# Gated attention stage: scores and gate as one product of 334 columns, key bias added on VectorE, mixing in two groups

## What is computed

```python
def _L1_xattn_ref(q, k, v, mask, Wq, bq, Wk, bk, Wv, bv, Wg, bg):
    q0 = q
    qp = q @ Wq + bq
    kp = k @ Wk + bk
    vp = v @ Wv + bv
    scale = 1.0 / jnp.sqrt(jnp.asarray(qp.shape[-1], qp.dtype))
    w = jnp.einsum('bqd,bkd->bqk', qp, kp) * scale
    w = jax.nn.softmax(w, axis=-1)
    x = jnp.einsum('bqk,bkd->bqd', w, vp)
    gate = jnp.concatenate((qp, x), axis=-1) @ Wg + bg
    x = x * mask[..., None]
    x = x * jax.nn.sigmoid(gate)
    return x + q0
```

## Time and profile before

| | us |
|---|---|
| median of the runs | 993.87 |
| span of the profiled execution | 989.4 |
| start of the last stage's first loads | 867.25 |
| the last stage, loads to end | 122 |
| TensorE, share of the span busy | 84% |
| VectorE / ScalarE / GpSimd | 68% / 43% / 47% |
| TensorE's mean granted clock | 0.909 |

### The profile page before, as it was taken

One profiled execution on the slowest core, in us unless ns is written; L12 is line 12 of the kernel. 1 busy time (PEld: TensorE's weight loads), 2 busy tenths in 40 slices (PEclk: granted clock), 3 DMA queues, 4 the chain that ended last, 5 costly groups with the idle time before them and its releaser, 6 DMA issues. The chain is left out here.

```text
span 989.4 us, 19663 instructions
## 1 busy us (share of the span) xinstructions
PE 831.0 (84%) x7264; PEld 678.2 (69%) x7264; DVE 677.2 (68%) x1459; ACT 430.4 (43%) x887; POOL 466.1 (47%) x584
## 2 busy tenths in 40 slices
PE   5974589998899988745778999989998989859997
PEld 4654467776677766434445888878877878859996
DVE  2633366766777776545689899999888887515664
ACT  3421135555555544422455555545443443234542
POOL 2003337766666764621234665655544556444440
PEclk9997799999999998856578999999999999958989
DMA  7293988796787771036435233323330000033333
GB/s 238 117 360 95 184 180 173 169 186 143 163 160 148 156 151 19 2 72 166 121 79 116 67 66 65 70 66 70 82 81 12 2 1 1 2 87 99 109 107 103
DMA packets 71102, 105.99 MB, mean 107 GB/s; under 512 B 21656, under 2 KB 60698, under 8 KB 66142
## 3 DMA queue, kind: packets, MB, share of 16 engines
q1 hardware_dynamic: 67092, 97.91, 42.4%
q10 hardware_dynamic: 3916, 6.83, 1.9%
HBM read 68.57 MB, written 35.62 MB: 105 GB/s over the span
## 5 line engine op out<-in xcount | busy, mean ns | idle before, releaser
L1329 DVE TENSOR_REDUCE a_nm<-a_s 128x2 f32<-128x512 f32 (+1 forms) x192 | 129.4, 681 | 86.2 <-PE a_s L1145 84.3
L1287 ACT ACTIVATE a_pT<-a_st 128x512 f32<-128x512 f32 x192 | 111.7, 594 | 111.1 <-PE a_st L1168 109.9
L975 POOL TENSOR_TENSOR c_hl<-c_hid,c_hh 128x256 fp32r<-128x256 f32 x128 | 95.0, 742 | 134.7 <-DVE c_hid L857 133.8
L686 ACT ACTIVATE c_pT<-c_st 77x512 f32<-77x512 f32 x128 | 76.0, 594 | 167.4 <-PE c_st L556 151.3
L606 PE MATMUL c_down<-c_w,c_hh 128*128 128x256 f32 x512 | 116.2, 295 | 2.9 <-DVE res L865 2.9
L1449 POOL TENSOR_SCALAR_AFFINE_SELECT a_pT<-a_pT 128x256 f32<-128x256 f32 (+1 forms) x192 | 89.7, 484 | 30.0 <-ACT a_pT L1287 29.7
L78 PE MATMUL c_up<-c_fxh,c_w 128*128 128x256 f32 x512 | 100.7, 289 | 0.7 <-DVE c_hid L857 0.6
L606 PEld LDWEIGHTS c_down<-c_w,c_hh 128*128 128x128 f32 x512 | 87.3, 191 | 18.0 <-issue 18.0
L1168 PE MATMUL a_st<-a_sq,a_sk 98*128 98x256 bf16 (+1 forms) x512 | 76.2, 253 | 16.0 <-DMA a_sq<-a_mT 11.6
L78 PEld LDWEIGHTS c_up<-c_fxh,c_w 128*128 128x128 f32 x512 | 79.9, 192 | 1.9 <-DVE c_hid L857 1.4
L857 DVE TENSOR_SCALAR c_hid<-c_up,ff_b_col 128x256 f32<-128x256 f32 x128 | 61.4, 480 | 26.2 <-ACT c_hh L706 26.1
(11 more groups left out here) (247 smaller groups left out, 2275.7 us busy)
## 6 DMA issues: line engine op xcount, KB each, us to landing
qk_parts<-a_parts SPq DMA_DIRECT2D x16, 768.0 KB
a_sq<-qk_parts SPq DMA_DIRECT2D x16, 384.0 KB, 5.3
a_sk<-qk_parts SPq DMA_DIRECT2D x16, 384.0 KB, 6.9
q_parts<-c_parts SPq DMA_DIRECT2D x16, 384.0 KB, 5.4
c_sq<-q_parts SPq DMA_DIRECT2D x16, 384.0 KB
g_vv<-vv_rows SPq DMA_DIRECT2D x16, 308.0 KB
vv_rows<-x_vv SPq DMA_DIRECT2D x9, 512.0 KB, 3.3
x<-in_xT SPq DMA_DIRECT2D x16, 256.0 KB, 9.4
```

The lines of the kernel that those rows point to most:

```text
L686: nc.scalar.activation(pT[g % NPT][:], st_ps[0:SC, :], ACT.Exp).then_inc(s_exp, 1)
L975: nc.gpsimd.tensor_tensor(hl[:, m, :], hid[n % NHID][:], f32(hh[:, m, :]), ALU.subtract).then_inc(s_hl, 1)
L1287: nc.scalar.activation(pT[g % NPT][:], st_ps[g % 2][:], ACT.Exp).then_inc(s_exp, 1)
L1329: nc.vector.tensor_reduce(nm[c % 2][:, QT * heads[0] + qt:QT * heads[-1] + qt + 1:QT], s_ps[g % 2][:].rearrange("p (h k) -> p h k", h=len( ...
```

## The change

1. Scores and gate become one product (`gates_and_scores`). The right-hand tile `wf` holds the gate's 256 columns and the folded keys' 78 side by side (`GS` = 334), three buffers, each with its own copy of the gate's matrix. 12 matmuls of 334 columns write one bank of a new PSUM tile `gs` for each half of the tokens. The product stands where `scores(n)` stood; `gates(n-1)` at the step's end is gone.
2. The keys' bias is no longer added by products. It is loaded into all partitions, unrounded, and VectorE adds it while it takes the scores out of PSUM into `s_sb`; `maxes` and `exps` read that copy.
3. `mix` writes two groups: 6 matmuls of 256 columns into `xo` (x), and 6 of 256 into the gate half of `gs`.
4. The waits follow the tiles: `gates_and_scores(n)` waits for gate_tanh(n-2), which reads the gate half of the same buffer of `gs`; the bias's add waits for exps(n-1). `ht` has one buffer in place of two.
5. The context stage no longer rounds the bias into two parts.

```diff
-    fold = [sb(f"fold{i}", [P, 2, KT, SCE], F32R) for i in range(ND)]
+    GS = D + SCE
+    wf = [sb(f"wf{i}", [P, 2, KT, GS], F32R) for i in range(ND)]
-    cb = sb("cb", [1, B, 2, SCE], F32R)
-    wqg = sb("wqg", [P, 2, KT, D], F32R)
+    cb = sb("cb", [P, B, SC], F32)
+    s_sb = sb("s_sb", [P, QT, SC], F32)
-    ht = [ps(f"ht{i}", 512) for i in range(2)]
-    sc, pt = ps("sc", 512), ps("pt", 512)
-    xo = [ps(f"xo{i}", QT * 2 * D) for i in range(2)]
+    ht, pt = ps("ht", 512), ps("pt", 512)
+    gs = [ps(f"gs{i}", QT * 512) for i in range(2)]
+    xo = [ps(f"xo{i}", 512) for i in range(2)]
...
-                sp.dma_start(f32(fold[c % ND][:].rearrange("p x k s -> p (x k s)")), d.fold[:, c]).then_inc(f_loaded[c % ND], 16)
+                sp.dma_start(f32(wf[c % ND][:, :, :, D:GS]), d.fold[:, c].rearrange("p (x k s) -> p x k s", x=2, k=KT)).then_inc(f_loaded[c % ND], 16)
...
+            def gates_and_scores(c):
+                if not real(c):
+                    return
+                if c < ND:
+                    pe.wait_ge(w_loaded[c], 16)
                 pe.wait_ge(s_xl, c + 1)
                 pe.wait_ge(f_loaded[c % ND], 16 * (c // ND + 1))
-                atleast(pe, s_exp, c)
+                atleast(pe, s_fact, c - 1)
                 for qt in range(QT):
-                    o = sc[:, qt * SCE:(qt + 1) * SCE]
-                    mm3(nc.tensor, o, lambda x, kt: (xh, xl)[x][c % 3][:, kt, qt * P:(qt + 1) * P], lambda y, kt: fold[c % ND][:, y, kt, :], range(KT),
-                        stop=False)
-                    mt(o, one[:], cb[:, c, 0, :], start=False, stop=False)
-                    last = mt(o, one[:], cb[:, c, 1, :], start=False, stop=True)
-                last.then_inc(s_sc, 1)
+                    last = mm3(nc.tensor, halves(gs[c % 2])[:, qt, 0:GS], lambda x, kt: (xh, xl)[x][c % 3][:, kt, qt * P:(qt + 1) * P],
+                               lambda y, kt: wf[c % ND][:, y, kt, :], range(KT))
+                last.then_inc(s_gs, 1)
...
-            def gates(c):
-                if not real(c):
-                    return
-                atleast(pe, s_gated, c - 1)
-                for qt in range(QT):
-                    last = mm3(nc.tensor, xo[c % 2][:, qt * 2 * D + D:(qt + 1) * 2 * D], lambda x, kt: (xh, xl)[x][c % 3][:, kt, qt * P:(qt + 1) * P],
-                               lambda y, kt: wqg[:, y, kt, :], range(KT))
-                last.then_inc(s_gates, 1)
...
+                atleast(pe, s_gated, c - 1)
                 for qt in range(QT):
-                    for i, (x, y) in enumerate(((0, 0), (1, 0), (0, 1))):
-                        last = mt(xo[c % 2][:, qt * 2 * D:(qt + 1) * 2 * D], (pth, ptl)[x][:, qt, :], vv[c % ND][:, y, :], start=False, stop=i == 2,
+                    shares = ((0, 0), (1, 0), (0, 1))
+                    for i, (x, y) in enumerate(shares):
+                        mt(xo[c % 2][:, qt * D:(qt + 1) * D], (pth, ptl)[x][:, qt, :], vv[c % ND][:, y, 0:D], start=i == 0, stop=i == 2,
+                           skip_group_check=True)
+                    for i, (x, y) in enumerate(shares):
+                        last = mt(halves(gs[c % 2])[:, qt, 0:D], (pth, ptl)[x][:, qt, :], vv[c % ND][:, y, D:2 * D], start=False, stop=i == 2,
                                   skip_group_check=True)
...
             for n in steps:
                 mix(n - 2)
-                scores(n)
+                gates_and_scores(n)
                 turn_p(n - 1)
                 turn_h(n + 1)
-                gates(n - 1)
...
-            act.dma_start(f32(wqg[:].rearrange("p x k c -> p (x k c)")), d.wqg).then_inc(w_loaded, 16)
-            act.dma_start(f32(cb[:].rearrange("o b x s -> o (b x s)")), d.cb).then_inc(w_loaded, 16)
+            for v, done in zip(wf, w_loaded):
+                act.dma_start(f32(v[:, :, :, 0:D]), d.wqg.rearrange("p (x k c) -> p x k c", x=2, k=KT)).then_inc(done, 16)
+            act.dma_start(cb[:].rearrange("p b s -> p (b s)"), d.cb[0].partition_broadcast(P)).then_inc(b_loaded, 16)
...
-                nc.scalar.activation(gate[c % 2][:], xo[c % 2][:].rearrange("p (q c) -> p q c", q=QT)[:, :, D:2 * D], ACT.Tanh, scale=0.5).then_inc(s_fact, 1)
+                nc.scalar.activation(gate[c % 2][:], halves(gs[c % 2])[:, :, 0:D], ACT.Tanh, scale=0.5).then_inc(s_fact, 1)
...
-                dve.wait_ge(s_sc, c + 1)
-                nc.vector.tensor_reduce(nmax[:], sc[:, 0:QT * SCE].rearrange("p (q k) -> p q k", q=QT)[:, :, 0:SC], AX.X, ALU.max,
-                                        negate=True).then_inc(s_max, 1)
+                if c == 0:
+                    dve.wait_ge(b_loaded, 16)
+                dve.wait_ge(s_gs, c + 1)
+                atleast(dve, s_exp, c)
+                nc.vector.tensor_tensor(s_sb[:], halves(gs[c % 2])[:, :, D:D + SC], cb[:, c, :].unsqueeze(1).broadcast_to([P, QT, SC]),
+                                        ALU.add).then_inc(s_biased, 1)
+                dve.wait_ge(s_biased, c + 1)
+                nc.vector.tensor_reduce(nmax[:], s_sb[:], AX.X, ALU.max, negate=True).then_inc(s_max, 1)
```

More of the change, by code:

```diff
@@ L175, in _ @@
             sp.dma_start(d.row, f32(row[:].rearrange("o x c -> o (x c)"))).then_inc(row_stored, 16)
-            sp.wait_ge(s_cbl, NC)
-            sp.dma_start(d.cb, f32(cb[:].rearrange("o b x s -> o (b x s)"))).then_inc(cb_stored, 16)
+            sp.wait_ge(s_cbf, NC)
+            sp.dma_start(d.cb, cbf[:]).then_inc(cb_stored, 16)
             for v in t.x_loaded:
@@ L351, in _ @@
                 nc.vector.tensor_scalar(cbf[:, c0:c0 + cn], kps[c % 2][0:1, 0:cn], cb0[:], SCALE, ALU.add, ALU.mult).then_inc(s_cbf, 1)
[L352 to L355, removed]
             dve.wait_ge(s_rowh, 1)
@@ L1509, in gated_attention @@
     fin = [sb(f"fin{i}", [P, QT, D], F32) for i in range(2)]
-    ht = [ps(f"ht{i}", 512) for i in range(2)]
-    sc, pt = ps("sc", 512), ps("pt", 512)
-    xo = [ps(f"xo{i}", QT * 2 * D) for i in range(2)]
-    names = ("nmr", "half", "onef", "one", "pad", "z", "zg", "h", "ht", "xh", "xl", "sc", "max", "exp", "rec", "p", "pt", "pth", "ptl", "gates", "xo", "fact", "gated", "fin")
-    (s_nmr, s_half, s_onef, s_one, s_pad, s_z, s_zg, s_h, s_ht, s_xh, s_xl, s_sc, s_max, s_exp, s_rec, s_p, s_pt, s_pth, s_ptl, s_gates, s_xo, s_fact, s_gated, s_fin) = (sem("g_" + n) for n in names)
-    w_loaded, row_loaded = sem("g_weights"), sem("g_row")
+    ht, pt = ps("ht", 512), ps("pt", 512)
+    gs = [ps(f"gs{i}", QT * 512) for i in range(2)]
+    xo = [ps(f"xo{i}", 512) for i in range(2)]
+    names = ("nmr", "half", "pad", "z", "zg", "h", "ht", "xh", "xl", "gs", "biased", "max", "exp", "rec", "p", "pt", "pth", "ptl", "xo", "fact", "gated", "fin")
+    (s_nmr, s_half, s_pad, s_z, s_zg, s_h, s_ht, s_xh, s_xl, s_gs, s_biased, s_max, s_exp, s_rec, s_p, s_pt, s_pth, s_ptl, s_xo, s_fact, s_gated, s_fin) = (sem("g_" + n) for n in names)
+    w_loaded, b_loaded, row_loaded = [sem("g_weights") for _ in range(ND)], sem("g_key_bias"), sem("g_row")
     f_loaded, v_loaded = [sem("g_fold") for _ in range(ND)], [sem("g_values") for _ in range(ND)]
@@ L1522, in gated_attention @@
     two = lambda v: v[:].rearrange("p (k s) -> p k s", k=KT)
+    halves = lambda v: v[:].rearrange("p (q c) -> p q c", q=QT)
     with nc.Block() as block:
@@ L1635, in x_high @@
                 act.wait_ge(s_ht, c + 1)
-                atleast(act, s_gates, c - 2)
-                nc.scalar.activation(xh[c % 3][:], two(ht[c % 2]), ACT.Copy).then_inc(s_xh, 1)
+                atleast(act, s_gs, c - 2)
+                nc.scalar.activation(xh[c % 3][:], two(ht), ACT.Copy).then_inc(s_xh, 1)
             def exps(c):
@@ L1644, in exps @@
                 for qt in range(QT):
-                    last = nc.scalar.activation(p_sb[c % 2][:, qt, 0:SC], sc[:, qt * SCE:qt * SCE + SC], ACT.Exp, bias=nmax[:, qt:qt + 1],
+                    last = nc.scalar.activation(p_sb[c % 2][:, qt, 0:SC], s_sb[:, qt, :], ACT.Exp, bias=nmax[:, qt:qt + 1],
                                                 accum_out=sums[:, qt:qt + 1])
@@ L1660, in gate_tanh @@
                 atleast(act, s_gated, c - 1)
-                nc.scalar.activation(gate[c % 2][:], xo[c % 2][:].rearrange("p (q c) -> p q c", q=QT)[:, :, D:2 * D], ACT.Tanh, scale=0.5).then_inc(s_fact, 1)
+                nc.scalar.activation(gate[c % 2][:], halves(gs[c % 2])[:, :, 0:D], ACT.Tanh, scale=0.5).then_inc(s_fact, 1)
             act.wait_ge(s_nmr, 1)
-            act.wait_ge(s_onef, 1)
-            nc.scalar.activation(one[:], onef[:], ACT.Copy).then_inc(s_one, 1)
             for n in steps:
@@ L1694, in x_low @@
                 dve.wait_ge(s_xh, c + 1)
-                nc.vector.tensor_tensor(xl[c % 3][:], two(ht[c % 2]), f32(xh[c % 3][:]), ALU.subtract).then_inc(s_xl, 1)
+                nc.vector.tensor_tensor(xl[c % 3][:], two(ht), f32(xh[c % 3][:]), ALU.subtract).then_inc(s_xl, 1)
             def p_low(c):
@@ L1707, in gate_x @@
                 atleast(dve, s_fin, c - 1)
```

(2 more changed lines are left out.)

26 lines of the change are left out of this document (8 added, 18 removed).

## The result

The changed kernel takes 1039.52 us, the median of four runs (1033.41 to 1047.14), beside 992.57 for the kernel before (989.14 to 996.11): a ratio of 1.048, 95% interval 1.040 to 1.055. The forecast was 1010.9, with 997 to 1030 as its range. The direction was right, the size was not: +47 us where +17 was forecast.

What follows compares the result with a forecast made beforehand. TensorE was taken to bound the last stage's steps, 6.35 us each. 13 steps +16.3, the step to the fifteenth mixing +1.2 and the start -0.5 made +17.0 on 993.87: 1010.9 us, range 997 to 1030.

Steps and rivals of the forecast that it cites:

- The bound of the kernel before, and what covers the line: TensorE sets the last stage's pace; transposes and gate product (2.19 us) cover the 2.05 us line from scores to mixing.
- The ring: Last stage's step sums product 2.10, line to mixing 2.40, mixing 1.67, tanh 0.68: 6.85 us at full clock.
- The price of 334 columns: In TensorE's joined product, 0.153 us for each matmul at full clock, 1.84 us for 12.
- The clock: Lower level for a third of the 13 steps' time: 7.6 us a step, +16.3 us (+6.5 to +42).
- Rival B: Waits in each step hold the last stage's clock down most of the time: +31 to +43, 1025 to 1037 us; chance 0.12.
- speeds add: Last stage's step from both clock levels: 1 / (0.667/6.85 + 0.333/9.6) = 7.6 us.
- The start: Last stage up to its first mixing: gain of 1.9 to 3.4 against load delay of 1.5, together -0.5 us.
- The tail: Step to the fifteenth mixing at 6.85 in place of 5.63 us: +1.2; last mixing and everything after: 0.
- Rival A: Wide products keep the last stage's clock full, steps of 6.85 us: +4 to +9, 998 to 1003 us; chance 0.27.
- Rival C: VectorE's bias add is blocked by GpSimd, the line up to 1.3 us longer: +23, 1017 us; chance 0.05.
- Rival D: Last stage's ring not closed, steps of 4.3 us as the busiest engine needs: -27, 967 us; chance 0.06.
- The parts at nothing: Single `ht` buffer, add's wait for exps(n-1), folded keys' shorter pieces, context stage: 0, at best -0.8 us.

Runs made afterwards that it cites:

- p_bias: Kernel before with only the bias moved to VectorE's add, its one-row products gone, scores and gate still two products: 981.74 us, 0.9885 of before.
- e_fill: Changed kernel with ten filler matmuls of 256 columns, 128 rows, in TensorE's waits of each step: 1006.97 us, 1.013 of before.
- e_nobias: Changed kernel without the add of the keys' bias, maximum and exponentials reading the scores from PSUM: 1008.19 us.
- e_fill2: Changed kernel with two filler matmuls in each step, behind the transposes: 1019.30 us.
- e_line: Changed kernel with the previous weights' high part ahead of ScalarE's exponentials and their low part ahead of VectorE's bias add: 1008.68 us, 1.018 of before.
- a0: Changed kernel without any edit, profiled a second time: 1039.49 us.
- e_biasearly: Changed kernel with the bias loaded second in ScalarE's queue, ahead of the gate matrix's second and third copy: 1030.83 us.
- e_best2: `e_order` with bias loaded second, norm behind tanh, VectorE's x split between maximum and division, turn_h ahead of turn_p: 967.31 us, 0.973 of before.
- e_order: Changed kernel with lists reordered: TensorE's transposes ahead of the wide product, splits of the weights ahead of exponentials and bias add: 979.66 us, 0.987 of before.
- e_thin: Changed kernel with ten fillers a step as in `e_fill`, but one active row in place of 128: 1045.53 us.

## Why the prediction was right and wrong

**The bound of the kernel before, and what covers the line:** right. `p_bias` took work from TensorE and the step went to 5.41, scores 1.28 + line 2.46 + mixing 1.67, as that reading demands.

**The ring:** right in every link, 7.01 us where 6.85 was worked out. The missing 0.16 are the exponentials from SBUF (0.36 each against 0.33) and 0.14 us from the tanh's end to the product, where I had put 0.05.

**The price of 334 columns:** (937.05 - 935.51) / 10 = 0.154 us in `e_fill`, forecast 0.153. The Trainium skill, page "TensorE: Matmul & The Clock Gate", section "Back-to-back issue gap", gives by its formula, which it says is for a single matmul by itself, 0.142; in this stream, where each matmul has its own weight load, the row is 8% above that.

**The clock: the step that failed.** I took a third of the time at the lower level between ends of none and all. It was 70%. Two rows stood before me: the stretch 420 to 530, with TensorE busy in 65% and the clock at 0.63, and the wide gate product in which the clock rose at the start. The first, which I called the nearest, was nearly the answer; I let the second pull it down by an argument with no number in it. And that argument misread its row: the stretch at the lower level held the bias's one-row products beside the scores' narrow ones, and `p_bias`, which keeps the narrow ones and drops those of one row, has a clock of 0.98, so that width held the level down isn't shown. Rival B had the right mechanism and nearly the size (three quarters at the lower level, +31, steps of 8.7; all of it, +43), and I gave it 0.12 and cut the range at 1030. With B's step and the start as measured the sum is 13 x (8.7 - 6.35) = 30.6, + (8.7 - 5.6) = 3.1 for the fifteenth, + 2.9 for the start: +37.

A second fault lies in the same term: "speeds add". With the measured 70% my formula gives 1 / (0.30/6.85 + 0.70/9.6) = 8.6 us, and the step took 9.07, 13 x 0.5 = 6 us more in all. The formula takes it that both levels meet the same mix of work and waits. They don't: in the 13 steps of the changed kernel TensorE had matmuls in 18.3 of the 36.0 us at full clock (51%) and in 70.1 of the 81.9 at the lower (86%). The product at 954.66 ran all at the lower level (3.69 us), and the full clock came at 958.51, into the 2.4 us in which TensorE waits for VectorE and ScalarE.

The runs show how badly "a third" was founded: at the ring's own length the share is 70% (both profiles), with a ring 0.42 us shorter 16% (`e_nobias`), and between them lie only `e_fill2` (0.80) and `e_line` (0.84), each moved there by an edit. Where a kernel stands so near an edge the range has to hold both sides of it.

**The start:** forecast -0.5, measured +2.9 (+2.2 in `a0`). TensorE stood idle 5.5 us ahead of the second product; 2.1 of them are left in `e_biasearly`, so the load's delay was some 3.4 us (2.2 in `a0`), not 1.5. I let all loads land at 883.5 by a rate, 16.3 us after the stage's first issue, and put the bias before that; it landed 15.2 us after its own issue, 17.3 after the first. And I left ScalarE's own issuing out: its first norm starts 4.2 us after its first issue, 2.4 before, since seven loads stand ahead of it where there were five (three copies of the gate's matrix in place of one), the bias's among them with 1.16 us.

```profile
881.31 0.70 ACTq L1603
882.04 1.16 ACTq L1604
...
884.23 1.10 ACT g_z L1614 x2
```

**The tail:** forecast +1.2, measured +4.7 over two steps and the end, at clocks of 0.80, 0.62 and 0.50, where I had full clock for all.

**Rival A** (the clock stays up) is refuted for the change and is what `e_fill` shows, with 12 us over the kernel before (1006.97 and 994.75 beside it). **Rival C:** the add takes 0.32 us in each of its 16 rows, and in the changed kernel none of them overlaps an operation of GpSimd, so this kernel doesn't put the rival to the test. `e_best2` does: 12 of its 16 adds overlap one, and each takes 0.32 us. The Trainium skill, page "SBUF — State Buffer", section "Who interferes with whom", says that a VectorE operation with at most one SBUF input, outside its two-port modes, doesn't contend with GpSimd, and that trace agrees. **Rival D** (no closed ring) needed another order, and there it came nearly true: `e_best2` steps at 4.39 to 4.6 (4.52 in the mean) against the 4.3 of its sum. The parts at nothing: the early stages are the same to 0.1 us in the mean, which shows no cost but couldn't show one under some 3 us; the single `ht` buffer and the shorter pieces of the folded keys appear in no wait of the changed kernel's steps.

## What to carry to other kernels

When work is taken out of a hand-ordered pipeline, look for what it covered: here a product that TensorE did "too much" hid a 2.4 us line through two other engines, and sharing a tile between a matmul and the activation that reads it added a wait that nothing in that order covered. Follow the new waits once round all the lists before counting work; if they close a ring, the step is its sum, and reordering the lists may be worth more than the saving. A ring with idle TensorE can pay in clock besides: here that was 19.4 us beside the ring's own 16.0, while `e_order`, with waits of its own, kept the full clock. A forecast near such an edge needs a range that holds both levels.

## What the runs showed of the hardware

The granted clock didn't follow the share of time in which TensorE was busy. At 95% with matmuls of one row in the waits it was 0.65 (1.2 GHz in 70% of the time), at 80% with the same matmuls of 128 rows 0.96, at 69% with a ring 0.42 us shorter 0.92. Two fillers a step, 0.24 us of work, made it 0.80. What the chip goes by wasn't measured beyond these rows; that the fillers' active rows made the difference, and not their time, rests on `e_fill` and `e_thin`, one run of the latter. Scatter: the unchanged early stages end within a range of 14 us; why wasn't looked into, and single profiles of this kernel can't be compared by their spans.
